# Graph network kernel: x turned early, own term in the eviction, layer norm folded into the u product, neighbour sum in column chunks

## What is computed

```
agg = segment_sum(x[src], dst)
h   = (1 + eps) * x + agg
h   = relu(batch_norm(h @ W1 + b1, g1, be1))      # 512 -> 1024, statistics over the nodes
h   = relu(batch_norm(h @ W2 + b2, g2, be2))      # 1024 -> 512
x1  = layernorm(x + (x + h))
u   = relu(x1 @ lw1 + lb1)                        # 512 -> 256
y   = u @ lw2 + lb2                               # 256 -> 512
out = layernorm(x1 + y + segment_sum(y[dst], src))
```

## Time and profile before

| | |
|---|---|
| median of 3 runs | 285.03 us (284.92 to 285.14) |
| profiled execution, its own time | 287.6 us |
| its span, first to last instruction | 285.8 us |
| busy: TensorE, VectorE, ScalarE, POOL | 259.5, 144.4, 123.0, 76.6 us |
| mean granted TensorE clock | 0.985 of 2.4 GHz |
| neighbour product on TensorE | 29.1 to 93.3 us |
| first product | 93.3 to 148.1 us |
| second product | 148.1 to 203.2 us |
| last product, first to last matmul | 265.35 to 279.7 us |
| half_in<-turns (turned blocks of A), median from issue to landing | 4.5 us |

### The profile page before, as it was taken

One profiled execution on the slowest core, in us unless ns is written; L12 is line 12 of the kernel. 1 busy time (PEld: TensorE's weight loads), 2 busy tenths in 40 slices (PEclk: granted clock), 3 DMA queues, 4 the chain that ended last, 5 costly groups with the idle time before them and its releaser, 6 DMA issues.

```text
span 285.8 us, 4044 instructions
## 1 busy us (share of the span) xinstructions
PE 259.5 (91%) x1581; PEld 221.6 (78%) x1581; DVE 144.4 (51%) x348; ACT 123.0 (43%) x217; POOL 76.6 (27%) x73
## 2 busy tenths in 40 slices
PE   0657999998999999999999999999769999999991
PEld 0636998886888888888888888888649888888770
DVE  1588997552743144444443313004474545448884
ACT  1407353424867047555556220200445445342694
POOL 5420000000920006565656700048301211112120
PEclk9999999999999999999999999999986999999998
DMA  4276000000056810000003795009000000000044
GB/s 139 93 277 240 0 2 0 2 0 6 2 203 236 274 42 1 2 0 0 2 20 126 254 234 102 0 19 202 11 1 2 1 0 2 0 0 2 3 180 175
DMA packets 21846, 20.43 MB, mean 71 GB/s; under 512 B 13911, under 2 KB 14846, under 8 KB 21826
## 3 DMA queue, kind: packets, MB, share of 16 engines
q1 hardware_dynamic: 21320, 19.91, 22.8%
q0 software_dynamic: 160, 0.13, 0.2%
q10 hardware_dynamic: 346, 0.10, 0.2%
HBM read 10.94 MB, written 5.92 MB: 59 GB/s over the span
## 4 chain that ended last, share of the span: by engine, by line
PE 81%; DVE 7%; ACT 5%; DMA 4%; issue 1%; DVEq 0%; SPq 0%; POOLq 0%
PE ps L1006 19%; PE ps L993 19%; PE ps L941 17%; PE ps L1078 7%; PE ps L1067 6%; PE ps L893 3%; PE ps L923 2%; PE ps L1052 2%; DVE hot_s L683 2%; PE ps L1125 2%; DMA src_i<-in_src 2%; PE ps L1043 1%; DMA pairs<-pair 1%; DMA run<-pairs,start_i 1%; PE ps L1064 1%
## 5 line engine op out<-in xcount | busy, mean ns | idle before, releaser
L758 DVE BATCH_NORM_STATS2 stats<-ps 128x6 f32<-128x500 f32 (+1 forms) x36 | 21.6, 599 | 63.1 <-PE ps L1006 35.2
L941 PE MATMUL ps<-AT,xh 128*128 128x500 f32 (+1 forms) x120 | 45.2, 385 | 0.0
L941 PE MATMUL ps<-AT,xl 128*128 128x500 f32 (+1 forms) x120 | 42.8, 364 | 0.0
L993 PE MATMUL ps<-h0h,wh 128*128 128x500 f32 (+1 forms) x96 | 34.0, 354 | 0.0
L993 PE MATMUL ps<-h0h,wl 128*128 128x500 f32 (+1 forms) x96 | 33.8, 352 | 0.0
L993 PE MATMUL ps<-h0l,wh 128*128 128x500 f32 (+1 forms) x96 | 33.7, 351 | 0.0
L443 ACT ACTIVATE AT<-ps 128x500 fp32r<-128x500 f32 x25 | 14.8, 590 | 32.3 <-PE ps L923 32.3
L941 PEld LDWEIGHTS ps<-AT,xl 128*128 128x128 f32 x120 | 24.3, 202 | 2.5
L941 PEld LDWEIGHTS ps<-AT,xh 128*128 128x128 f32 x120 | 24.2, 202 | 2.5
L1006 PE MATMUL ps<-a1h,wl 128*128 128x500 f32 (+1 forms) x96 | 24.9, 354 | 0.0
L1006 PE MATMUL ps<-a1l,wh 128*128 128x500 f32 (+1 forms) x96 | 24.8, 354 | 0.0
(11 more groups left out here) (141 smaller groups left out, 528.8 us busy)
## 6 DMA issues: line engine op xcount, KB each, us to landing
turns<-half_out SPq DMA_DIRECT2D x10, 320.0 KB, 2.2
xs<-in_x SPq DMA_DIRECT2D x1, 2304.0 KB
out<-xs SPq DMA_DIRECT2D x9, 256.0 KB
w1s<-in_L_gnn_W SPq DMA_DIRECT2D x1, 2048.0 KB, 10.4
w2s<-in_L_gnn_W SPq DMA_DIRECT2D x1, 2048.0 KB, 8.3
xs<-in_x SPq DMA_DIRECT2D x1, 1280.0 KB, 7.9
xs<-in_x SPq DMA_DIRECT2D x1, 1024.0 KB
lws<-in_L_gnn_W SPq DMA_DIRECT2D x1, 512.0 KB, 3.6
```

Of the source, the lines that this page charges most:

```text
L758: link(nc.vector.bn_stats(stats[:, 6 * c:6 * c + 6], ps[:, zbank(t, c), 0:c1 - c0]))
L941: last = mm(o, part[0:r, k, d * P:d * P + P], AT[0:r, k, c0:c1], start=False, stop=(k == NT - 1 and j == 1), skip_group_check=True)
L993: last = mm(ps[:, zbank(t, c), 0:c1 - c0], w[:, t, d * P:d * P + P], h[c][:, d, :], start=(d == 0 and j == 0), stop=(d == DT - 1 and j == 2))
```

## The change

**x is turned once, early.** TensorE transposes the ten blocks of x (`x_cols`, L968): five at the start, five between the second build and the flag's branch. ScalarE copies them to xT (`x_turn`). `own`, `diag` and `keep_warm` are gone. VectorE adds the own term into the PSUM bank after the item's sum (`h0_own`, L728); `h0_high` waits for that, one, two and three slots behind for own, high and low part.

**The layer norm is folded into the u product.** ScalarE's ReLU of the second batch norm goes to a32, VectorE updates xT to 2x+h (`xp_sum`), still with features on partitions, and that is split into xph and xpl and multiplied with lw1, whose column means are taken off (`lw1_sum`, one fp32 matmul on TensorE, `lw1_center`). The per-node scale and the bias lb1 come in `u_scale`; the ReLU is taken in the split (ScalarE for the high, POOL for the low part). x1 itself comes from `xp_rows` (L1118), whose transposition is evicted by the apply (L598). u needs three of four feature blocks before the last batch norm is done (`hidden_early`), the fourth after it (`hidden_last`).

**The neighbour sum** v runs in three column chunks of 512, 512 and 226 (`neighbours`, L1131), and the last product's blocks (`second`, L1149) stand between them. w2 comes in eight pieces through four buffers; x is not loaded a second time; lw2 and six of the ten turned blocks are asked for after the last z_sum. The second product's last block is no longer done by chunks, so all three statistics follow its end.

```diff
+        y_banks = (4, 5, 6, 7, 0)
+        def u_at(k):
+            return ps[0:rows[k], k // 2, k % 2 * L:k % 2 * L + L]
+
+        def x_bank(k):
+            return 3 + k % half
+        v_before = {2: 1, 6: 2}
...
+        OWN_LAG, HIGH_LAG, LOW_LAG = 1, 2, 3
+
+        def h0_after(g):
+            return [i for i, k in slot_units[g] if k == NT - 1] if g >= 0 else []
...
-            sp.dma_start(w2s[:, :, :], w2.rearrange("(k p) n -> p k n", p=P)).then_inc(w2_in, 16)
-            sp.wait_ge(z_sum, HT)
-            sp.dma_start(lws[:, :, :], lw1.rearrange("(k p) n -> p k n", p=P)).then_inc(lw_in, 16)
-            sp.dma_start(lw2s[:, :, :], lw2.rearrange("(k p) n -> p k n", p=P)).then_inc(lw_in, 16)
+            sp.wait_ge(half_set, NT)
+            for k in range(HT):
+                if k >= W2R:
+                    sp.wait_ge(w2l_set, k - W2R + 1)
+                sp.dma_start(w2s[k % W2R][:, :], w2[P * k:P * k + P, :]).then_inc(w2_in[k % W2R], 16)
+            sp.wait_ge(a1l_last, 1)
+            sp.dma_start(lws[:, :, :], lw1.rearrange("(k p) n -> p k n", p=P)).then_inc(lw1_in, 16)
             for i in range(ATS):
                 sp.wait_ge(spilled[i], 16 * cdiv(NT - i, ATS))
-            sp.wait_ge(w2h_set, HT)
             sp.wait_ge(w2l_set, HT)
-            sp.dma_start(xs[:, 0:NT - 1, :], x[0:full, :].rearrange("(t p) d -> p t d", p=P)).then_inc(x_again, 16)
-            sp.dma_start(xs[0:rows[-1], NT - 1, :], x[full:N, :]).then_inc(x_again, 16)
             for k in range(NT):
                 b = k % len(half_in)
+                if k == len(half_in):
+                    sp.wait_ge(z_sum, BT)
+                    sp.dma_start(lw2s[:, :, :], lw2.rearrange("(k p) n -> p k n", p=P)).then_inc(lw2_in, 16)
                 if k >= len(half_in):
                     sp.wait_ge(A_set, k - len(half_in) + 1)
                 sp.dma_start_transpose(half_in[b][:, :, :], turns[:, P * k:P * k + P]).then_inc(turned[b], 16)
...
+            def xp_low(d):
+                pl.wait_ge(xph_set, d + 1)
+                nc.gpsimd.tensor_tensor(xpl[:, d, :], xT[:, d, :], xph[:, d, :].bitcast(F32),
+                                        ALU.subtract).then_inc(xpl_set, 1)
...
-                if k == 8:
-                    pl.wait_ge(z_part, len(CH))
+                if k == len(half_in):
+                    pl.wait_ge(z_sum, BT)
...
+                nc.gpsimd.tensor_scalar(u32[0:r, k % UR, :], u32[0:r, k % UR, :], 0.0, None, ALU.max).then_inc(ur_set, 1)
+                pl.wait_ge(ur_set, k + 1)
+                nc.gpsimd.tensor_tensor(ul[0:r, k, :], u32[0:r, k % UR, :],
+                                        uh[0:r, k, :].bitcast(F32), ALU.subtract).then_inc(ul_set, 1)
...
+            def x_turn(k):
+                r = rows[k]
+                act.wait_ge(x_turned, k + 1)
+                nc.scalar.activation(xT[:, :, P * k:P * k + r],
+                                     ps[:, x_bank(k), :].rearrange("p (d c) -> p d c", c=P)[:, :, 0:r],
+                                     ACT.Copy).then_inc(xT_set, 1)
...
-                act.wait_ge(h0_sum, i + 1)
+                act.wait_ge(h0_own_set, i + 1)
...
                     if half + g < NT:
                         x_high(half + g)
-                    for i in items_after[g]:
+                        x_turn(half + g)
...
+            def xp_high(d):
+                if d == 0:
+                    act.wait_ge(z_sum, HT)
+                act.wait_ge(xp_set, d + 1)
+                nc.scalar.activation(xph[:, d, :], xT[:, d, :], ACT.Copy).then_inc(xph_set, 1)
+
+            for d in range(DT):
+                affine(HT + d)
+                xp_high(d)
+                if d == 1:
+                    act.wait_ge(lw1c_set, 1)
+                    act.wait_ge(w2l_set, HT)
+                    nc.scalar.activation(lw1h[:, :, :], lws[:, :, :], ACT.Copy).then_inc(lw1h_set, 1)
...
+                nc.scalar.activation(x1[0:r, k, :], ps[0:r, 5 + k % 2, :], ACT.Identity, bias=ln_r[0:r, k, 1:2],
                                      scale=ln_r[0:r, k, 0:1]).then_inc(x1_set, 1)
...
+            act.wait_ge(z_sum, BT)
             for s in range(NT + 2):
-                if 0 <= s - 1 < NT:
-                    xt_high(s - 1)
                 if s < NT:
                     ln_root(s)
-                    ln_apply(s)
+                if 0 <= s - 1 < NT:
+                    ln_apply(s - 1)
                 if 0 <= s - 2 < NT:
-                    u_relu(s - 2)
-            for i, b in enumerate(v_order):
+                    u_high(s - 2)
+                if s == half:
+                    act.wait_ge(lw2_in, 16)
+                    nc.scalar.activation(lw2h[:, :, :], lw2s[:, :, :], ACT.Copy).then_inc(lw2h_set, 1)
...
+            def h0_own(i):
+                c, d = divmod(i, DT)
+                c0, c1 = CH[c]
+                v.wait_ge(h0_sum, i + 1)
+                if i == 0:
+                    v.wait_ge(xT_set, NT)
+                o = ps[:, 2 + i % RING, 0:c1 - c0]
+                nc.vector.scalar_tensor_tensor(out=o, in0=xT[:, d, c0:c1], scalar=eps1[:, 0:1], in1=o,
+                                               op0=ALU.mult, op1=ALU.add).then_inc(h0_own_set, 1)
...
             for j in range(DT):
                 for k in range(j * each, min(NT, (j + 1) * each)):
                     loops(k)
+                h0_own(NI - DT + j)
                 h0_low(NI - DT + j)
...
+            def xp_sum(d):
+                v.wait_ge(act_set, 2 * (HT + d) + 2)
+                nc.vector.scalar_tensor_tensor(out=xT[:, d, :], in0=xT[:, d, :], scalar=2.0, in1=a32[0][:, :],
+                                               op0=ALU.mult, op1=ALU.add).then_inc(xp_set, 1)
+
+            def lw1_sum():
+                v.wait_ge(lw1_in, 16)
+                nc.vector.tensor_reduce(u32[:, 0, :], lws[:, :, :].rearrange("p d n -> p n d"), AX_X, ALU.add
+                                        ).then_inc(lsum_set, 1)
+
+            def lw1_center():
+                v.wait_ge(lmean_set, 1)
+                nc.vector.tensor_tensor(lws[:, :, :], lws[:, :, :], ps[:, 0, None, 0:L].broadcast_to([P, DT, L]),
+                                        ALU.subtract).then_inc(lw1c_set, 1)
+
+            def lw1_low():
+                v.wait_ge(lw1h_set, 1)
+                nc.vector.tensor_tensor(lw1l[:, :, :], lws[:, :, :], lw1h[:, :, :].bitcast(F32),
+                                        ALU.subtract).then_inc(lw1l_set, 1)
+
+            for d in range(DT):
+                batch_norm(HT + d)
+                xp_sum(d)
+                if d == 0:
+                    lw1_sum()
+                if d == 1:
+                    lw1_center()
+                if d == 2:
+                    lw1_low()
+            v.wait_ge(xph_set, DT)
+            nc.vector.tensor_tensor(xpl[:, DT - 1, :], xT[:, DT - 1, :], xph[:, DT - 1, :].bitcast(F32),
+                                    ALU.subtract).then_inc(xpl_last, 1)
...
+            def u_scale(k):
+                r = rows[k]
+                v.wait_ge(u_sum, k // 2 + 1)
+                if k == 0:
+                    v.wait_ge(lb1_in, 16)
+                if k >= UR:
+                    v.wait_ge(ul_set, k - UR + 1)
+                nc.vector.scalar_tensor_tensor(out=u32[0:r, k % UR, :], in0=u_at(k), scalar=ln_r[0:r, k, 0:1],
+                                               in1=lb1_all[0:r, :], op0=ALU.mult, op1=ALU.add).then_inc(u32_set, 1)
+
+            for s in range(NT + 2):
                 if s < NT:
                     ln_stats(s)
-                    ln_scale(s, ln_std_s, ln_aff)
-                if s >= 1:
-                    xt_low(s - 1)
+                if s >= 2:
+                    u_scale(s - 2)
+                if s < NT:
+                    ln_scale(s)
...
-            def own(i, k0=0, k1=NT):
-                c, d = divmod(i, DT)
-                c0, c1 = CH[c]
-                if i >= RING:
-                    pe.wait_ge(h0l_set, i - RING + 1)
-                for k in range(max(k0, c0 // P), min(k1, cdiv(c1, P))):
-                    a, b = max(c0, P * k), min(c1, P * k + P)
-                    mm(ps[:, 2 + i % RING, a - c0:b - c0], xs[0:rows[k], k, d * P:d * P + P],
-                       diag[0:rows[k], a - P * k:b - P * k], start=(a == c0), stop=False, skip_group_check=True)
-
+            def x_cols(k):
+                r = rows[k]
+                pe.wait_ge(*((x_in, 16) if k < half else (x_in2, 32)))
+                if k >= half:
+                    pe.wait_ge(xT_set, k - half + 1)
+                for d in range(DT):
+                    last = nc.tensor.transpose(ps[:, x_bank(k), d * P:d * P + r], xs[0:r, k, d * P:d * P + P],
+                                               ident[0:r, 0:r])
+                last.then_inc(x_turned, 1)
...
+            for k in range(half, NT):
+                x_cols(k)
...
+                if t == HT + 1:
+                    pe.wait_ge(mean_set, 1)
```

(40 more changed lines are left out.)

473 lines of the change are left out of this document (202 added, 271 removed).

## The result

The changed kernel takes 291.34 us (median of 4 runs, 288.55 to 293.62) beside 285.08 for the kernel before in the same runs; the ratio is 1.0155, with a 95% interval of 1.0095 to 1.0216. In a later set the untouched copy took 291.38 us (12 runs, 286.24 to 294.02) beside 286.04. Such a ratio leaves out every run over 1.5% above its kernel's fastest, in the copy 7 of 12, and would call the copy 0.5% slower (1.0054, 0.9999 to 1.0109); since the clocks of those 7 (0.919 to 0.942) lie among those of the rest (0.923 to 0.950), I take them for the kernel's own spread and compare medians of all runs. By these the changed kernel is 6.3 us slower than before (2.2%) and the copy 5.3. I had forecast 284.3 us, 0.7 faster, with a range of 278.8 to 288.6; the median lies above it.

The account below looks back on a forecast made before the run. TensorE, 81% of the chain, was taken as the bound, moving to a vector-engine chain late in the kernel. Own term and start -1.0, stop's clock +1.7, second product +0.4, final stretch -1.8: -0.7, so 284.3 us; range 278.8 to 288.6.

Parts of the forecast that it names:

- After Z: -1.8: From the last product's remaining statistics to the kernel's end: 80.7 us forecast against 82.5 before, 1.8 us saved.
- Z: The moment the last product's remaining statistics begin, 203.28 us in the kernel before.
- The start: Before the neighbour product: twenty transpositions at half speed move its start from 29.10 to 31.2, +2.1 us, bounds 0.8 and 3.4.
- Own term, stop and clock: Around the neighbour product's end: 1.0 of 7.4 us saved arrives, TensorE stands 3.5 us, the clock's fall costs 1.7.
- The clock's price, 1.7: After TensorE's stop near 93 us: the granted clock falls to 1.2 GHz, +1.7 us, between 0 and 3.3.
- The cycle: Row blocks after Z: transposition, statistics, root and apply take 2.9 us a block, 3.2 at 1.2 GHz.
- The end of u: First column chunk's end: last two blocks wait for scale, high part and POOL's two steps; chunk ends at Z+47.
- the third rival: POOL's widenings hold up VectorE's xT update and last low part: +2.0 us, 286.3 us, chance 0.12.
- Low clock lasts: Rival: TensorE's clock stays low longer after the stop near 93 us (+1.6) and between blocks (+2.5): 288.4 us, chance 0.21.
- VectorE blocked: Rival: POOL's widenings hold up VectorE's xT update and last low part, +2.0 us: 286.3 us, chance 0.12.
- My bound of 49 for the first chunk: Latest end forecast for the first column chunk, Z+49, if the low clock lasts to its end.
- the 0.2%: Whole kernel: a measurement was claimed to tell about 0.2% (0.6 us) from no change.

Follow-up runs that it names:

- all four edits: Changed kernel with pieces of h0 ahead of the copies, x1 updates late, apply behind its own root, low part of u on VectorE: 273.23 us, ratio 0.9558.

## Why the prediction was wrong

The step that failed is the term "After Z: -1.8", and in it the stretch from the last turned block to the end of the first column chunk: two engines in each other's way, and their wait not in the sum. The start was wrong too, but little of that reached the end.

**The start: wrong, mostly hidden.** Forecast +2.1 us, neighbour product from 31.2 on; it began at 29.38 (29.17 in the copy). The twenty transpositions took 4.31 us, 0.21 each, as the row said, at a granted clock of 0.50; but they began at 21.0, not at about 22, and from their end to the product were 4.1 us, not the 4.9 of my sum over both queues. In the other profiles that distance is 3.9 to 4.1 too, while the transpositions took 3.3 to 4.3 us and the product began at 28.25 to 29.89: the sooner the clock rose, the sooner it began (granted 0.96 in 23 to 25 in the soonest, 0.50 in the changed kernel).

**Own term, stop and clock: right.** The third chunk was to start at 96.4; it did at 95.82 and 96.34. TensorE arrived earlier than I thought (the product ended at 87.3, not 88.8, since it began earlier) and so stood longer, 4.3 us, not 3.5: the queue of copies mostly set the time, as the text said. The clock's price, 1.7, measured 1.6 to 2.4. Z was to come at 203.28 - 1.0 + 1.7 + 0.4 = 204.4 and came at 204.75. That it came so close has some luck in it: the third chunk began 0.6 us early, and from there to Z it took 0.9 us more than I had. What I took as given was that copies and pieces must alternate; one reordering is worth 4 to 5 us.

**After Z: the step that failed.** "After Z: -1.8" measured +4.6: 87.05 us, not 80.7 (the 80.7 is itself 0.2 short of the 80.9 that the terms give). By the marks of the forecast, in us behind Z:

| | forecast | measured | lost on the way |
|---|---|---|---|
| statistics of block 0 | 10.1 | 11.3 | 1.2 |
| transposition of block 2 | 13.9 | 14.8 | -0.3 |
| transposition of block 6 | 26 | 26.8 | -0.1 |
| transposition of block 9 | 38.1 | 40.0 | 1.1 |
| first column chunk done | 47 | 52.8 | 3.9 |
| end | 80.7 | 87.05 | 0.5 |

- *Block 0*: both long VectorE instructions met a widening and took 2.17 and 2.18 in place of 1.46; I had allowed 0.5 for both. Whether they meet one depends on when the turned block lands: of the ten profiles of versions that do not hold the widenings back, five have both instructions long, two have one and three neither. This is the third rival, and the rule of the Trainium skill that stood beside it, at the size of 1.4 us.
- *The cycle* was sized nearly right: four cycles from block 2 to 6 took 12.1 us, as forecast.
- *The end of u*, where most went: 12.8 us from the transposition of block 9 to the chunk's end, not 8.9. "POOL's two steps each" stand in the forecast without a delay of their own; the maximum took 0.85, most subtractions 0.73 and one 3.18, because VectorE, done with its own part, went on to the x1 updates in its program. I looked for POOL in VectorE's way and not for VectorE in POOL's. The low clock at 252 to 256 came behind that wait, and with the updates late it was 1.00 there.
- *From the chunk's end on* the count of matmuls held to half a microsecond.

**The rivals.** "Low clock lasts", 288.4: the clock was low, but full clock over four blocks gave 0.2 to 0.5 us in the profile and none in the median. "VectorE blocked", 286.3: the right mechanism, half of its reach. My bound of 49 for the first chunk came from the clock alone; it should have held a blocked POOL. And the 0.2% that a measurement was to tell from no change came from three runs that happened to agree: 29 runs of before lie 3.9 us apart, the copy's twelve 7.8.

**What I did not see.** The text says that block k+2 waits for k's apply "which stands behind k+1's root", and takes it as the cycle. It is an order of two lines, and with the apply behind its own root the cycle is 1.9 us, and in that run the clock held to 240 us. The change moved the bound from TensorE to this chain, and the chain had not been ordered for it.

Open: how much of the 9.3 us of that edit is the order on ScalarE and how much that on VectorE, which were moved together; and how much the widenings cost in runs rather than in profiles, where they met VectorE in some and not in others; and what the queue sum at the start had too long.

## What to carry over

When a change takes work off the bounding engine, read the other engines' programs as orders, not as durations: here each of four small edits, three of pure order and one that moved a step to another engine, was worth some 4 to 9 us alone, and together they turned 2% slower into 4% faster. Ask of every long VectorE instruction with SBUF inputs that is put "where there is room" what POOL is doing then, and of every POOL step at a chain's end the same. Before fighting a low TensorE clock, ask whether TensorE's waits set the time; with the apply behind its own root the clock stayed at 1.00 where it had needed warming before, though with all four edits it fell once more, to 0.61 over 4 us.
